# A ring of seven weight buffers, cosine tables made in mid-layer, and new slots, in a six-layer windowed-attention kernel

## The reference

```python
def attn_layer(x, Wqkv, qs, ksc, Wo):
    q, k, v = jnp.split(x @ Wqkv, 3, -1)      # 16 heads of 64
    q, k = l2norm(q) * qs, l2norm(k) * ksc
    q = q * cos * scale + rotate_half(q) * sin * scale
    k = k * cos * inv + rotate_half(k) * sin * inv
    return local_attention(q, k, v) @ Wo       # windows of 32 tokens, each sees itself and the one before
for i in range(DEPTH):                         # 6
    x = attn_layer(shift_tokens(x), Wqkv[i], ...) + x
    x = ffn_layer(shift_tokens(x), ...) + x    # layer norm, a * gelu(gate) up, down
```

## Time and profile before

| what | value |
|---|---|
| median of 3 runs | 1968.74 us (1967.22 to 1971.82) |
| profiled execution, its own time | 1972.55 us |
| its span, first to last instruction | 1971.2 us |
| busy share: PE, ACT, DVE, POOL | 95%, 81%, 80%, 54% |
| mean granted clock of PE | 0.981 of full speed |

### The profile page before, as it was taken

The page is one execution under the profiler, slowest core; times in us unless marked ns, Lnnn a source line. Parts: engine busy times, 40 slices in busy tenths (PEclk is TensorE's granted clock), DMA queues, the critical chain, the costliest instruction groups (busy, mean ns, idle before and its releaser), DMA issues.

```text
span 1971.2 us, 77005 instructions
## 1 busy us (share of the span) xinstructions
PE 1864.6 (95%) x34029; PEld 1569.4 (80%) x34029; DVE 1579.2 (80%) x2229; ACT 1596.0 (81%) x2751; POOL 1071.6 (54%) x523
## 2 busy tenths in 40 slices
PE   6999999869999999999999999999999999999987
PEld 4889898757887788887888788887888887888876
DVE  4556665588988888989898898988897988888873
ACT  2678887667887888888988889897888888898864
POOL 4100000267667666777676765758665667666530
PEclk9999999989998999999999999999999999999998
DMA  5000000033334334343443433343433334333331
GB/s 175 12 7 5 5 7 7 2 93 98 101 96 122 96 99 116 93 121 98 121 114 104 117 102 107 107 114 97 117 101 105 100 107 119 109 101 97 96 101 36
DMA packets 120101, 173.88 MB, mean 88 GB/s; under 512 B 25591, under 2 KB 44634, under 8 KB 119770
## 3 DMA queue, kind: packets, MB, share of 16 engines
q1 hardware_dynamic: 119596, 168.92, 30.6%
q10 hardware_dynamic: 174, 0.05, 0.0%
HBM read 117.54 MB, written 51.38 MB: 86 GB/s over the span
## 4 chain that ended last, share of the span: by engine, by line
PE 62%; POOL 12%; DVE 10%; ACT 8%; issue 7%; DMA 0%; ACTq 0%; POOLq 0%; SPq 0%; DVEq 0%
PE o_pair L758 7%; POOL rt L1672 7%; PE bank L706 6%; PE bank L838 5%; PE s_pair L728 5%; PE bank L683 5%; PE bank L685 4%; PE bank L684 4%; POOL rt L1663 4%; PE bank L610 4%; PE bank L740 3%; DVE bank L1466 3%; PE bank L860 2%; DVE t L1479 2%; PE bank L772 1%
## 5 line engine op out<-in xcount | busy, mean ns | idle before, releaser
L1672 POOL TENSOR_TENSOR rt<-rt,t 128x2048 f32<-128x2048 f32 x96 | 440.0, 4584 | 169.5 <-DVE t L1479 165.4
L1663 POOL TENSOR_TENSOR rt<-raw,rot 128x1024 f32<-128x1024 f32 x192 | 456.3, 2377 | 43.8 <-DVE rot L1451 11.8
L683 PE MATMUL bank<-wqkv_hi,xs 128*128 128x512 f32 x576 | 258.0, 448 | 15.2 <-ACT vn L1036 11.8
L1487 DVE TENSOR_TENSOR rt<-rt,bank 128x2048 f32<-128x2048 f32 x96 | 219.7, 2288 | 37.1 <-POOL rt L1672 35.2
L1019 ACT ACTIVATE raw<-bank 128x512 f32<-128x512 f32 x384 | 223.6, 595 | 26.7 <-PE bank L685 14.5
L758 PEld LDWEIGHTS o_pair<-pT,v 64*64 64x64 f32 x12288 | 198.2, 137 | 45.1 <-issue 20.7
L685 PE MATMUL bank<-wqkv_hi,xs 128*128 128x512 f32 x576 | 231.1, 401 | 0.0
L684 PE MATMUL bank<-wqkv_lo,xs 128*128 128x512 f32 x576 | 230.9, 401 | 0.0
L1479 DVE TENSOR_TENSOR t<-raw,bank 128x1024 f32<-128x1024 f32 x192 | 225.2, 1214 | 0.6
L758 PE MATMUL o_pair<-pT,v 64*64 64x32 f32 x12288 | 215.5, 222 | 10.5 <-issue 8.8
L1466 DVE TENSOR_REDUCE bank<-t 128x32 f32<-128x2048 f32 x96 | 219.5, 2287 | 5.7 <-ACT t L1027 3.0
(11 more groups left out here) (400 smaller groups left out, 4328.3 us busy)
## 6 DMA issues: line engine op xcount, KB each, us to landing
v<-v_rows SPq DMA_DIRECT2D x288, 256.0 KB, 4.4
v_rows<-vn SPq DMA_DIRECT2D x192, 256.0 KB, 3.6
v<-v_rows SPq DMA_DIRECT2D x96, 192.0 KB, 3.2
wraw<-in_L_ffn_Wqkv_dram SPq DMA_DIRECT2D x36, 256.0 KB, 2.9
wo<-in_L_ffn_Wo_dram SPq DMA_DIRECT2D x24, 128.0 KB
wraw<-in_L_ffn_W_in_dram SPq DMA_DIRECT2D x8, 256.0 KB, 2.7
w_out<-in_L_ffn_W_out_dram SPq DMA_DIRECT2D x8, 256.0 KB, 3.1
wraw<-in_L_ffn_W_dram SPq DMA_DIRECT2D x12, 170.5 KB, 2.8
```

The source lines that it names most:

```text
L683: pe.matmul(bank[:, :], hi, w[0][:, :], start=True, stop=False)
L1663: e = pool.tensor_tensor(heads(k.rt_r[c][:, part]), heads(k.raw_r[c][:, part]), cosv, ALU.mult)
L1672: pool.tensor_tensor(k.rt_r[c][:, :], k.rt_r[c][:, :], k.t2[:, :], ALU.add).then_inc(s["rot_add"], 1)
```

## The change

1. `wqkv` has seven pairs of tiles instead of six. Chunk n of layer l lies in pair (6 l + n) mod 7, so chunk n of the next layer takes the pair of chunk n-1 of this one, and chunk 0 takes a pair that has been free for a layer.
2. `layer_tables` is split. `cos_table(l + 1)` runs on DVE behind the last residual (`z_out`) of the layer's sample 2. `sin_table(l)` stays where the tables were. POOL's `cos0` waits for `cos_table` only.
3. All slot tables are replaced.
4. SP's `store_values` waits for the loads of two units before, and `load_gain` also waits for `cos_table`.

```diff
-        self.wqkv = [[sb(f"wqkv{n}_{part}", [P, 512], F32R) for part in ("hi", "lo")] for n in range(WCHUNKS)]
+        self.wqkv = [[sb(f"wqkv{n}_{part}", [P, 512], F32R) for part in ("hi", "lo")]
+                     for n in range(WCHUNKS + 1)]
...
+    def weights(self, l, n):
+
+        return self.wqkv[(WCHUNKS * l + n) % (WCHUNKS + 1)]
...
-            w = k.wqkv[n]
+            w = k.weights(l, n)
...
-POOL_AT = dict(xs=40, zero=60, w0=70, cos0=74, w1=74, add0=74, w2=74, w3=76, cos1=82, add1=82, w4=97, w5=101, w6=185,
-               w7=209)
+POOL_AT = dict(xs=4, zero=8, w0=15, cos0=40, w1=41, add0=43, w2=46, w3=46, cos1=57, add1=59, w4=68, w5=77, w6=159,
+               w7=173)
...
-    def layer_tables(l):
+    def halves_of(table):
+        return table.rearrange("p (h d) -> p h d", h=2)
+
+    def gain_of(l, n):
+        dve.wait_ge(s[f"ld_gain{l % 2}"], 32 * (l // 2 + 1))
+        return halves_of(k.gain[:, n, :])
+
+    def cos_table(l):
         src = k.cst("rot").rearrange("p (c k d) -> p c k d", c=TC, k=4)
-        dve.wait_ge(s[f"ld_gain{l % 2}"], 32 * (l // 2 + 1))
+        if l >= 2:
+            dve.wait_ge(s["rot_cos"], 2 * B * (l - 1))
+        for n in range(2):
+            g = gain_of(l, n)
+            for c in range(TC):
+                e = dve.tensor_tensor(halves_of(k.rot[l % 2][:, c, n, :]), halves_of(src[:, c, 2 * n, :]), g, ALU.mult)
+        e.then_inc(s["cos_table"], 1)
+
+    def sin_table(l):
+        src = k.cst("rot").rearrange("p (c k d) -> p c k d", c=TC, k=4)
         if l == 0 and k.rot_bank_freed:
             dve.wait_ge(*k.rot_bank_freed)
...
+        for n in range(2):
+            g = gain_of(l, n)
+            for c in range(TC):
+                e = dve.tensor_tensor(halves_of(k.rot_sin[:, c, n, :]), halves_of(src[:, c, 2 * n + 1, :]), g[:, ::-1, :],
+                                      ALU.mult)
         e.then_inc(s["tables"], 1)
...
         yield from t.to("sin0")
+        if u == 0:
+            cos_table(0)
         if b == 0:
-            layer_tables(l)
+            sin_table(l)
         rotate(0)
...
+        if b == 2 and l + 1 < DEPTH:
+            cos_table(l + 1)
...
-            hi, lo = k.wqkv[n]
-            if l and n < 4:
-                pool.wait_ge(s["pe_qk"], 8 * (B * l - 1) + 4 + n + 1)
+            hi, lo = k.weights(l, n)
+            if l and n == 0:
+                if l >= 2:
+                    pool.wait_ge(s["pe_v"], 4 * B * (l - 1))
+            elif l and n <= 4:
+                pool.wait_ge(s["pe_qk"], 8 * (B * l - 1) + 4 + n)
             elif l:
-                pool.wait_ge(s["pe_v"], 4 * (B * l - 1) + 2 + n - 4 + 1)
+                pool.wait_ge(s["pe_v"], 4 * (B * l - 1) + 2 + n - 4)
...
             if b == 0 and c == 0:
-                pool.wait_ge(s["tables"], l + 1)
+                pool.wait_ge(s["cos_table"], l + 1)
...
         def store_values(c, r):
+            if c == 0 and r == 0 and u >= 2:
+                for n in range(TC):
+                    sp.wait_ge(s[f"v2_{n}"], pair_count(2 * (u - 2) + n))
```

More of the change, by code:

```diff
@@ L163 @@
 EXPERTS_START, EXPERTS_SPACING = 70, 40
[L164 removed]
+LATE_START, LATE_SPACING = 376, 32
 PE_A = dict(ln_sq_a=6, ln_sd_a=6, ln_out_a=14, features=20, k_features=27, q_features=35, sums=39, kv_turn=43,
@@ L194 @@
-DVE_AT = dict(ss0=32, sin0=41, nrm0=52, ss1=52, sin1=54, nrm1=68, smax0=79, ssum0=89, smax1=93, ssum1=109, z_mid=138,
-              xc=142, hn=150, hh0=164, hh1=164, hh2=164, z_out=182)
-POOL_AT = dict(xs=40, zero=60, w0=70, cos0=74, w1=74, add0=74, w2=74, w3=76, cos1=82, add1=82, w4=97, w5=101, w6=185,
-               w7=209)
-SP_AT = dict(gain=22, w0=71, w1=84, w2=89, w3=89, st00=94, st01=94, st10=97, st11=97, w4=107, pair00=109, pair01=119,
-             w5=126, pair10=126, pair11=146, wo=180, w6=196, w7=213, w2d=240)
+PE_AT = dict(qk00=29, qk01=29, qk02=29, qk03=29, qk10=38, qk11=42, qk12=52, qk13=52, v00=58, v01=61, v10=63, v11=63,
+             tqk00=65, tqk01=69, tqk02=74, tqk03=74, tqk10=75, tqk11=75, s00=75, tqk12=75, tqk13=77, s01=77, s10=89,
+             tp00=98, tp01=98, s11=100, a00=103, a01=105, tp10=119, tp11=119, a10=125, a11=125, wo=139, mean=141,
+             var=154, up0=167, up1=168, up2=168, down=185)
@@ new lines @@
+ACT_AT = dict(xs=2, qk00=25, qk01=25, qk02=25, qk03=25, sq0=30, qk10=31, norm0=38, qk11=38, qk12=43, qk13=47, sq1=47,
+              norm1=56, v00=56, v01=57, v10=58, v11=58, tqk00=60, tqk01=63, tqk02=69, tqk03=69, tqk10=74, tqk11=74,
+              tqk12=74, tqk13=74, exp0=86, tp00=94, tp01=94, exp1=105, tp10=114, tp11=114, o0=114, o1=121, xf=138,
+              lnsq=139, rstd=148, gelu0=160, gelu1=160, gelu2=161)
+DVE_AT = dict(ss0=33, sin0=39, nrm0=53, ss1=53, sin1=58, nrm1=71, smax0=78, ssum0=92, smax1=95, ssum1=108, z_mid=136,
+              xc=142, hn=154, hh0=163, hh1=163, hh2=163, z_out=182)
@@ L201 @@
+POOL_AT = dict(xs=4, zero=8, w0=15, cos0=40, w1=41, add0=43, w2=46, w3=46, cos1=57, add1=59, w4=68, w5=77, w6=159,
+               w7=173)
+SP_AT = dict(gain=5, w0=33, w1=74, w2=79, w3=79, st00=79, st01=81, st10=88, st11=88, w4=88, pair00=90, pair01=107,
+             w5=107, pair10=119, pair11=128, wo=166, w6=201, w7=201, w2d=222)
 SIGNALS = (
@@ L208 @@
     "pe_spT spT pe_at1 at1 pe_atT x3 "
-    "zpad zero_kv xs_hi xs_lo tables pe_qk raw sq sq_sum ss rot_cos rot_sin rot_add norm nrm pe_qkT qkT pe_v vn pe_s smax exp "
+    "zpad zero_kv xs_hi xs_lo tables cos_table pe_qk raw sq sq_sum ss rot_cos rot_sin rot_add norm nrm pe_qkT qkT pe_v vn pe_s smax exp "
     "ssum pe_pT pT pe_o oT pe_wo z_mid xf ln_mean ln_xc ln_sq ln_var ln_sd hn pe_w1 gelu hh pe_w2 z_out "
@@ L1436, in experts @@
         yield from layer_norm(t, b, "d", k.mcol(1, 4, b), k.mcol(1, 3, b), k.z(b))
-    def layer_tables(l):
-        src = k.cst("rot").rearrange("p (c k d) -> p c k d", c=TC, k=4)
-        dve.wait_ge(s[f"ld_gain{l % 2}"], 32 * (l // 2 + 1))
+    def halves_of(table):
[4 more added lines that the diff above has]
+    def cos_table(l):
+        src = k.cst("rot").rearrange("p (c k d) -> p c k d", c=TC, k=4)
+        if l >= 2:
[7 more added lines that the diff above has]
+        src = k.cst("rot").rearrange("p (c k d) -> p c k d", c=TC, k=4)
         if l == 0 and k.rot_bank_freed:
             dve.wait_ge(*k.rot_bank_freed)
-        if l >= 2:
-            dve.wait_ge(s["rot_cos"], 2 * B * (l - 1))
-        for c in range(TC):
-            for n in range(2):
-                g = k.gain[:, n, :].rearrange("p (h d) -> p h d", h=2)
-                half = lambda t: t.rearrange("p (h d) -> p h d", h=2)
-                dve.tensor_tensor(half(k.rot_sin[:, c, n, :]), half(src[:, c, 2 * n + 1, :]), g[:, ::-1, :], ALU.mult)
-                e = dve.tensor_tensor(half(k.rot[l % 2][:, c, n, :]), half(src[:, c, 2 * n, :]), g, ALU.mult)
+        for n in range(2):
[3 more added lines that the diff above has]
+                                      ALU.mult)
         e.then_inc(s["tables"], 1)
@@ L1749, in load_gain @@
             sp.wait_ge(s["tables"], l)
+            sp.wait_ge(s["cos_table"], l)
         for j, n in enumerate(("q", "k")):
```

9 lines of the change are left out of this document (removed).

## The result

| | before | changed |
|---|---|---|
| median | 1970.28 us (4 runs, 1967.22 to 1975.16) | 1998.20 us (4 runs, 1997.63 to 2005.21) |
| ratio to before, 95% interval | | 1.0148 (1.0116 to 1.0179) |
| profiled execution, span | 1971.2 us | 2003.9 us |
| mean granted clock | 0.981 | 0.970 |

The changed kernel is slower, by 27.9 us. The forecast was 1997 with a range of 1976 to 2012. Its profiled execution (2005.21 us) is 7.0 us above its median, so 32.7 us of difference in the spans are more than the medians have.

What follows compares the result with a forecast made beforehand. The prediction took PE as full, with the POOL and DVE loop as long as the period. 1972.55 + 8.8 + 10.0 - 0.5 + 10.4 = 2001.25 us profiled, less 3.81 to the median: 1997, range 1976 to 2012.

Steps and rivals of the forecast that it cites:

- The hold: At both tables: a small DVE instruction reading SBUF twice waits until POOL's running instruction is over.
- three rows behind the prediction's reading: Earlier trace: L1450 (up to 756 ns), L1341 (0.96 us) and L1392 (3.98 us), read as DVE waiting for POOL.
- three terms: Losses forecast for the sine table at a layer's start, +8.8 us, the cosine table in mid-layer, +10.0, and the clock, +10.4.
- Sine table, +8.8: Layer's start: sine table held behind POOL's pair, 2.0 us at two changes of layer and 1.6 at three, +8.8 us.
- Cosine table, +10.0: Mid-layer, sample 2: cosine table held until `cos1` ends, delaying `add1` by 1.4 to 2.3 us in five places, +10.0 us.
- Clock, +10.4: Ten places where PE stands longer: four extra falls of the granted clock at 2.6 us each, +10.4 us.
- argument of the loop: Whole unit: the POOL and DVE loop is as long as the period, so a late sine part delays all behind it.
- Covered edits: Moved split of chunk 0, SP's later loads and added waits, and `load_gain`: all 0, bounds 0 to +1 us.
- late exponential: ACT's c = 1 exponential, behind four copies: 0 by 0.6 us of margin; rival with it late about 2010, chance 0.04.
- Before layer 0, -0.5: Ahead of the first rotation: cosine table made earlier, the 0.7 us wait shrinks; -0.5 us, bounds -2 and +2.
- Not held, faster: Rival: no table is held; waits go (-11.1), cosine costs 3.2 and sine 0.5: -7.5 us, 1961, chance 0.12.
- Only one half is held: Rival: cosine not held, +14 us, 1983; or sine slips through instead, about 1975; chance 0.14.

Runs made afterwards that it cites:

- ring and slots alone: Changed kernel with its ring of seven and all slots, but both tables made at a layer's start and `cos0` waiting for both: 1968.2 us, ratio 1.0008.
- no hold: Changed kernel with `cos0` waiting for the sine table too, and chunk 0's split and SP's load of chunk 2 put back: 1965.3 us, ratio 0.9997.
- the cosine hold alone: Changed kernel with POOL's `cos0` waiting for the sine table too: 1972.6 us, ratio 1.0040.
- the sine hold alone: Changed kernel with chunk 0's split back behind `add1` and SP's load of chunk 2 moved back too: 1990.0 us, ratio 1.0114.
- split-alone run: Changed kernel with only chunk 0's split put back behind `add1` of sample 6, SP's load left early: 2017.9 us, ratio 1.0258.
- run 20: Not a run's number: the 20 belongs to "20 us slower", said of the split-alone run, which measured 2017.9 us, ratio 1.0258.
- version with PSUM: Changed kernel with the gain copied to PSUM, where both tables read it: 1956.9 us, ratio 0.9960; timed again 1958.8 us, 0.9954.
- version with the cosine table in PSUM: Changed kernel in which only the cosine table reads its gain from a PSUM copy, the sine table from SBUF: 1993.2 us, ratio 1.0123.

## Why the prediction was right

**The hold: right, in both places.** Table instructions beside a working POOL took up to 2.39 and 1.78 us instead of 0.22, whether they write to PSUM or to SBUF, and none did once one input was in PSUM, though POOL worked beside all of them. The Trainium skill's rule (page "SBUF — State Buffer", section "Who interferes with whom") goes by the two SBUF inputs of the DVE instruction, against a GpSimd instruction that reads SBUF, and by which of them issues first. The traces agree with both parts. The rule doesn't name the output, and here it made no difference: the sine table's goes to PSUM, the cosine table's to SBUF.

What POOL does matters too. Ahead of layer 0 in the changed kernel all eight table instructions ran beside POOL's memsets, which read nothing, and none was held. DVE and POOL:

```profile
381.65 0.63 DVE L1468 TENSOR_TENSOR bank<-const,gain 128x64 f32<-128x64 f32 x4
381.69 1.09 POOL L1665 MEMSET v<- 32x512 f32 x2
```

One of the three rows behind the prediction's reading is of another kind than it says. L1392 (3.98 us) reads one SBUF tile and a constant, not SBUF twice, and yet it ended at 393.96 with POOL's `add0` (389.39 + 4.54 = 393.93), in the kernel before:

```profile
389.39 4.54 POOL L1672 TENSOR_TENSOR rt<-rt,t 128x2048 f32<-128x2048 f32 x1
```

So two SBUF inputs are not the only way into such a delay; no run here looks for the other one.

**What PE's time says of the three terms.** PE multiplies the same in both kernels (34029 recorded products). So the time in which it stands shows the stalls, and the time in which it is busy grows only where it works more slowly. The sums over the five A, before and changed, and over the five B, before and changed (length, then busy us of each engine, PE first):

```profile
sum 165.32, PE 156.12 PEld 128.89 DVE 139.26 ACT 138.56 POOL 119.45; mean PE 31.22 PEld 25.78 DVE 27.85 ACT 27.71 POOL 23.89
sum 179.26, PE 161.06 PEld 131.43 DVE 149.70 ACT 138.98 POOL 118.22; mean PE 32.21 PEld 26.29 DVE 29.94 ACT 27.80 POOL 23.64
sum 172.64, PE 163.94 PEld 135.49 DVE 144.39 ACT 138.09 POOL 138.80; mean PE 32.79 PEld 27.10 DVE 28.88 ACT 27.62 POOL 27.76
sum 188.07, PE 169.25 PEld 141.51 DVE 160.74 ACT 138.20 POOL 135.51; mean PE 33.85 PEld 28.30 DVE 32.15 ACT 27.64 POOL 27.10
```

PE stands 9.2 us in the five A before and 18.2 after, 9.0 more; in the five B 8.7 and 18.8, 10.1 more. Its busy time in both grows by 10.2. The forecast had 10.0, 8.8 and 10.4. (Some products move across the ends of A and B, so the single sums are good to about 1 us. Over all of the first five layers PE stands 16.3 us more, and is busy for 12.4 more with the same products.)

**Sine table, +8.8: right mechanism, size near.** PE stands 10.1 us more, 1.9 to 2.2 in each layer, for a forecast of 2.0 and 1.6. The start times were right (POOL 0.53 ahead, 0.6 forecast; DVE done at 1161.2, 5.03 after POOL's start, 5.2 forecast). PE's first wait grew from 0.56 to 3.88, and the second one, of 1.12, is gone: 3.88 - 1.68 = 2.2 more, the value that the prediction worked out beside the 2.0 that it took. B grew by 3.1 and not by 2.2 in layer 2 because PE is also busy for 31.96 us instead of 31.07, at a granted clock of 0.95 (before, then changed):

```profile
1123.43:1156.34 32.91, 31.07 (x658) 25.50 (x652) 28.88 (x40) 27.54 (x47) 27.78 (x14) 1.00 0.42 115
1139.40:1175.40 36.00, 31.96 (x632) 26.53 (x628) 32.29 (x36) 27.60 (x46) 27.21 (x14) 0.95 0.38 105
```

So even the smallest B of the changed kernel holds some of the clock's cost.

**Cosine table, +10.0: right in three layers, luck in the sum.** Four instructions took 2.16, and what follows them starts 2.0 later in layers 0, 1 and 3, for a forecast of 1.4, 2.05 and 2.3 there. Unheld they cost 0.6 (A 33.6 against 33.0), so the hold itself is 1.4 of each 2.0. In layers 2 and 4, A is 38.0 and 36.2, but it is 38.4 and 35.6 with ring and slots alone: there the table fell into a stall of PE that the prediction did not have, and added next to nothing. (The five parts of the term add up to 10.1, not 10.0.)

**Clock, +10.4: right as a sum over A and B, not as a count of falls.** PE's busy time grew by 10.2 us there, and by 12.4 over the first five layers as a whole. Between 500 and 1890 us, 18 stretches of 8 us had a granted clock under 0.97 against 6 before. Four falls at 2.6 each were a price taken from one pair of layers, and that the product fits is partly luck: the kernel before has falls of its own in B (PE busy for 163.9 us), which ring and slots alone don't have (155.4 at 1.00 in the one profile), and against these the changed kernel's B costs 13.8 by the clock.

**Which hold costs what.** Four runs undo neither, one or both. By their ratios: no hold 0.9997, the cosine hold alone 1.0040, the sine hold alone 1.0114, both 1.0142. So the sine hold costs some 20 to 23 us with the clock that it takes down, and the cosine hold, with the earlier split and load, 5.5 to 8.5, each difference uncertain by 4 to 6 us. The total of the forecast is right; the share of the sine table's place in it, clock included, is larger than the terms make it seem.

**The median.** The forecast for the profiled execution was 28.7 us more than before, and it was 32.7, of which 3.3 lie outside A and B, mostly in the last layer (3.0), for which the prediction had no term. The medians are 27.9 apart, as the changed kernel's profiled execution was 7.0 above its median and the one before 3.8 above the median of its first three. That the forecast is within 1 us of the median is luck, that it is within the range is not.

**A misread row.** Of the earlier trace rows the prediction says that POOL has 27.6 and ACT 25.8 us of the unit. By the columns 27.64 is ACT's, 20.04 POOL's, and 25.82 is PE's weight load. POOL is thus idle for a third of the unit. The argument of the loop goes by start times and waits and stands without these figures.

**Covered edits: right as a sum, but not each for itself.** Ring, slots and the late exponential give 1.0008. I priced SP's queue by its waits for value loads and said nothing of the chunk load that waits for POOL's split. That tie makes the split-alone run 20 us slower than the changed kernel. The stall of PE in layers 2 and 4 was not foreseen either.

**Before layer 0, -0.5:** the first `z_out` is 0.9 later; within its bounds.

**The rivals.** "Not held, faster" was 7.5 us below the kernel before, and the version with PSUM is 7.7 to 9.0 below it: its sum was sound, and its condition false. "Only one half is held" is the version with the cosine table in PSUM, 1.0123 or some 24 us above the kernel before where 14 was worked out for it. The sum had one fall of the clock, 2.6; PE's busy time in A and B grew by 10.5 there.
